# Softmax attention: value products of two key tiles in one block, and a third buffer for the exponentials

## The reference

```
qkv = x @ qkv_w.T + qkv_b          # q, k, v: 16 heads x 2048 x 8
p   = softmax(q @ k.T / sqrt(8))
out = (p @ v) @ proj_w.T + proj_b
x   = x + out
```

## Time and profile before

| | us |
|---|---|
| median of 3 runs | 1849.06 |
| lowest and highest | 1844.62, 1851.38 |
| the profiled execution | 1840.17 |
| its span | 1838.4 |
| mean granted clock of PE | 0.928 |

### The profile page before, as it was taken

How to read it: one execution, slowest core, us unless ns; L and a number is a source line. 1 busy time by engine, 2 the same in 40 slices (tenths; PEclk the granted TensorE clock), 3 DMA queues, 4 the chain that set the end, 5 groups by cost and what they waited for, 6 DMA issues and landing times. The chain is left out here.

```text
span 1838.4 us, 21584 instructions
## 1 busy us (share of the span) xinstructions
PE 1607.5 (87%) x7285; PEld 675.5 (37%) x7285; DVE 1352.3 (74%) x1951; ACT 856.2 (47%) x1493; POOL 222.4 (12%) x145
## 2 busy tenths in 40 slices
PE   6987589999999999999998799899984446589999
PEld 3433212222222222222223344466651112266665
DVE  5775798888888888888851777556666999745554
ACT  2443417777777777777776434322223000132221
POOL 2222300000000000000000122211100334201110
PEclk8998659999999999999999999899996767799999
DMA  6000310011001100120000000000000000000000
GB/s 171 4 0 1 124 30 8 15 28 37 12 15 28 33 15 15 28 32 10 2 2 1 1 0 0 1 1 0 0 1 0 0 1 0 1 1 6 6 6 7
DMA packets 32017, 29.42 MB, mean 16 GB/s; under 512 B 7789, under 2 KB 27033, under 8 KB 31929
## 3 DMA queue, kind: packets, MB, share of 16 engines
q1 hardware_dynamic: 31928, 28.31, 6.1%
HBM read 22.13 MB, written 4.19 MB: 14 GB/s over the span
## 5 line engine op out<-in xcount | busy, mean ns | idle before, releaser
L1350 DVE TENSOR_REDUCE mx<-ps 128x1 f32<-128x1024 f32 x512 | 603.1, 1219 | 108.9 <-PE ps L1262 107.6
L1338 ACT ACTIVATE xT<-ps 128x512 f32<-128x512 f32 x512 | 277.8, 598 | 123.4 <-PE ps L1285 117.0
L1262 PE MATMUL ps<-k,q 72*128 72x512 bf16 x1024 | 324.0, 399 | 11.0 <-DVE mx L1350 9.3
L1285 PE MATMUL ps<-q,k 84*128 84x512 bf16 x1024 | 311.7, 383 | 8.9 <-ACT xT L1338 6.4
L1338 ACT ACTIVATE xn<-ps 128x512 f32<-128x512 f32 x512 | 278.1, 601 | 83.9 <-PE ps L1285 79.1
L1285 PEld LDWEIGHTS ps<-q,k 84*128 84x128 bf16 x1024 | 96.4, 97 | 372.7 <-ACT xn L1338 152.6
L854 ACT ACTIVATE silu<-ps 128x512 f32<-128x512 f32 x144 | 85.3, 596 | 265.2 <-PE ps L827 261.8
L889 DVE TENSOR_TENSOR hid<-ps,silu 128x512 f32<-128x512 f32 x144 | 97.8, 689 | 90.2 <-PE ps L831 88.5
L827 PE MATMUL ps<-xT,ew 128*128 (+1 forms) x288 | 150.4, 604 | 6.4 <-PEq L1718 4.8
L817 PEld LDWEIGHTS ps<-ew,hid 128*128 128x128 f32 x1152 | 138.7, 192 | 30.6 <-issue 29.9
L831 PE MATMUL ps<-xT,ew 128*128 (+1 forms) x288 | 148.8, 599 | 0.0
(11 more groups left out here) (239 smaller groups left out, 1686.2 us busy)
## 6 DMA issues: line engine op xcount, KB each, us to landing
k<-k_parts SPq DMA_DIRECT2D x90, 64.0 KB
q<-q_parts SPq DMA_DIRECT2D x144, 32.0 KB
k<-k_parts SPq DMA_DIRECT2D x108, 32.0 KB
ew<-in_L_ffn_w_dram SPq DMA_DIRECT2D x2, 1024.0 KB
wraw<-in_L_ffn_w_dram SPq DMA_DIRECT2D x3, 512.0 KB, 6.7
q_parts<-part SPq DMA_DIRECT2D x4, 384.0 KB, 3.9
k_parts<-part SPq DMA_DIRECT2D x4, 384.0 KB, 2.6
v<-values SPq DMA_DIRECT2D x8, 144.0 KB, 6.1
```

What stands on the lines that cost most here:

```text
L1262: mm = nc.tensor.matmul(m.ps[:, S1B[2 * (i % 2) + kc % 2], :], queries, k1[:, h, kc * CHUNK:(kc + 1) * CHUNK], start=True, stop=True)
L1285: nc.tensor.matmul(m.ps[:, S2B[n % len(S2B)], :], k2[:, h, kt * P:(kt + 1) * P], q[:, qc, h, :], start=True, stop=True).then_inc(s2_ready, 1)
L1338: nc.scalar.activation(ex[kt % P_RING][:, h, :], m.ps[:, S2B[n % len(S2B)], :], ACT.Exp)\
L1350: nc.vector.reduce_max(mx[:, h, qt, kc:kc + 1], m.ps[:, 2 * (i % 2):2 * (i % 2) + 2, :], AX.XY)\
```

## The change

PE no longer runs a value block behind every tile but behind every odd tile, and then those of the two tiles one after the other. The exponentials get a third buffer, `ex2`, with memory of its own (four heads x 512 numbers per partition), and the buffer of a tile is now its running number over all units modulo 3, where it was the tile's number modulo 2. The copy of a unit's result on ACT stands behind the fourth exponential of the next unit's tile 0, not behind the third. Everything else, the first pass, the number of matmuls, the three PSUM banks of the scores and all transfers, stays as it is.

```
-P_RING = 2
+P_RING = 3
...
         ex = [m.xT[:, :].rearrange("p (h t) -> p h t", t=CHUNK),
-              m.xn[:, :, :].rearrange("p (h a) d -> p h (a d)", a=TPC)]
+              m.xn[:, :, :].rearrange("p (h a) d -> p h (a d)", a=TPC),
+              m.sb("ex2", [P, GH, CHUNK], stack=stack)]
...
                     last = nc.tensor.matmul(m.ps[32 * h:32 * h + VC, AVB, :], v[:, kt, h, :],
-                                            ex[kt % P_RING][:, h, :], start=(kt == 0), stop=(kt == TILES - 1),
+                                            ex[(u * TILES + kt) % P_RING][:, h, :], start=(kt == 0), stop=(kt == TILES - 1),
...
                     score(n + 5)
                     score(n + 6)
                     ahead(u, 2 * kt + 1)
-                    weigh(u, kt)
+                    if kt % 2 == 1:
+                        weigh(u, kt - 1)
+                        weigh(u, kt)
...
-                        nc.scalar.activation(ex[kt % P_RING][:, h, :], m.ps[:, S2B[n % len(S2B)], :], ACT.Exp)\
+                        nc.scalar.activation(ex[(u * TILES + kt) % P_RING][:, h, :], m.ps[:, S2B[n % len(S2B)], :], ACT.Exp)\
                             .then_inc(exped, 1)
-                        if kt == 0 and h == 2 and u > 0:
+                        if kt == 0 and h == 3 and u > 0:
                             store_out(u - 1)
```

## The result

The change made the kernel slower: 1880.82 us (median of 4 runs, 1874.44 to 1885.0) against 1846.84 (1841.06 to 1851.38), ratio 1.018, 95% interval 1.0146 to 1.0222. The profiled execution, at 1885.0 us the slowest of the four, has a span of 1883.2 us against 1838.4, mean granted clock 0.92 against 0.928.

What follows compares the result with a forecast made beforehand. PE's stream and ACT's exponential loop were both taken as close to binding, ACT's loop binding in the last 20 tiles. Terms summed to +24.7 us: 1864.9 against the profiled 1840.17, 1873.8 against the median 1849.06; range 1862 to 1890.

Steps and rivals of the forecast that it cites:

- the sum: All loop terms added: units 0 to 13 19.0, unit 14 to tile 11 1.2, last 20 tiles 4.5; together +24.7 us.
- rival B: Between two value blocks: the second block's weights are loaded in the open, +15 us, 1889; chance 0.13.
- The pair in the middle: Two tiles in the middle of a unit: 5.79 us against 5.64, +0.15 per pair.
- both waits: In a middle pair: first pass waits for DVE's reduction until 2.15 (costs 0.18), score 10 for exponential 7 until 3.19 (0.17).
- The unit: One unit's pairs added: 6 x 0.15 + 0.32 + 0 + 0.15 = 1.37 us more.
- tiles 12 and 13: Pair beside the empty first-pass slot: ends at 5.63 us, change 0.
- The seam: Place between two value blocks: bounds nothing or up to 0.12 us for eight weight loads; taken as nothing.
- Rival A: PE's stream alone sets the time: each pair 0.20 to 0.22 us shorter, -27 us, 1822; chance 0.09.
- Rival D: Third buffer doesn't do its work, ACT stands in the double block: 25 us more, 1899; chance 0.05 including the unseen.
- The copy: Start of a unit: copy before exponential 4 shifts everything up to score 10 by 0.33 us; difference +0.15.
- The last 20 tiles: Tiles without first pass, bound by ACT's loop: pair 5.19 us against 4.76, +0.43 for each of 10 pairs.
- score 6's: Before the change, score 6 waits for exponential 3: weights load at 1.08 us, just in time for its turn at 1.10.

Runs made afterwards that it cites:

- cut kernels: Kernel before (single blocks) and changed kernel (pairs), both with half of each exponential and reduction left out: 1820.88 us, ratio 0.9865, and 1792.08 us, ratio 0.9722.

## Why the prediction was right, and where it was short

It said 1873.8 us, range 1862 to 1890, slower; measured 1880.82. By the ratio the loss is 1.84% or 34 us (27 to 41), where the sum had 24.7. The account of the middle of the units came out to a few hundredths. That the total fell inside the range is in part luck: the sum was short by 9 us, and the range reached that far up only to take in rival B, which is false.

- *The pair in the middle.* 5.79 forecast, 5.79 in the trace, with both waits at their places (2.15 and 3.19 forecast, 2.14 and 3.19 found). The mechanism, the meeting of PE's stream with ACT's loop, is what the runs with shortened ACT and DVE show: pairs save 28.2 us against single blocks once both are out of the way.
- *The unit.* 1.37 us forecast, 1.44 found; tiles 12 and 13, taken at nothing, cost 0.05.
- *The seam.* Taken at nothing; it is nothing, the second block starts 0.86 to 0.87 behind the first. Rival B falls.
- *Rival A* (PE's stream alone, faster) fell as well, though its premise is true: 0.22 us per visit saved, against the 0.20 read from the gaps at entry and exit. The drain at a change of tiling mode that the Trainium skill speaks of (TensorEngine Tiling (Array Packing), Key Properties) agrees with the 0.22 us that the two cut kernels show per visit, though no run tells a drain from another cost of the change. The gain that follows from it alone did not come.
- *Rival D* (no help from the third buffer) did not apply, but its price was about right: 6.01 per pair measured without the buffer, and about 32 us above the changed kernel where 25 was written.
- *The copy.* Forecast to cost 0.33 us where it now stands; moving it back gave 0.29.
- *The last 20 tiles: the term that was mis-sized.* I wrote +0.43 for each of 10 pairs, at the clock of 1.00 that the earlier trace rows show. The first two pairs are at 5.20, as forecast. Then one takes 7.32 (with the copy in it) and six take 6.84, 1.64 us longer still, because the clock fell with PE's longer waits. That is about 11 of the 14.5 us by which the profiled loops (39.2) exceed the sum. How much of it an execution pays varies: the four of the changed kernel took 1885.0 and 1883.51 us at mean clocks of 0.920 and 0.921, and 1878.13 and 1874.44 at 0.925, while with single blocks in these tiles all four lay between 1867.8 and 1869.42. I had read the clock before the change and kept it for a stretch in which PE now waits longer at a time. The row has PE at 43.2 of 49 us there, where it was 99.0 of 100 in the middle, and that should have made a rival of it.
- *The start.* Before unit 0's copy 2.3 us more were lost than forecast. The first pair's two value blocks ran at 1.2 GHz (1.7 each), and the stretch from 270 to 280 has a clock of 0.55 against 0.93. No run tested this apart, but the profiles speak for a later rise with pairs. Where no work is left out, the granted clock goes to 1.00 54.4 to 56.7 us after the fill of `k` in the five kernels with single blocks, and 57.8 to 59.7 us after it in the five with pairs, one profile each. The loops up to the first copy took 97.8 to 99.3 us with single blocks and 100.4 or more with pairs, of which the copy's place makes up to 0.8. In the cut kernels the rise came equally early with both orders (50.1 and 49.4 us).
- *What holds ACT's loop in the last 20 tiles.* The prediction took the trace to show ACT's emptying of PSUM as the limit there. With seven banks and scores issued further ahead, a tile fell from 2.38 to 1.96 us with exponentials as long as before. So what held these tiles was that with three banks no score could be ready earlier, and not ACT's rate; ACT was busy 41.0 of 49 us.

Of the 44.8 us between the two profiled spans, 5.6 lie outside the loops. The fill of `k` started anywhere from 215.3 to 223.1 us in the kernels profiled, which are the same up to there. What sets it stays open.

## What to carry to other kernels

When an engine is 99% busy, a saving on it helps only as far as the engines that feed it can keep up with the shorter time: put the producers' loop and the engine's stream on one time axis and see which wait is just met, as score 6's was (1.08 against 1.10). Batching work that used to give a producer time to catch up asks for a deeper ring (more buffers in rotation) between the two, here PSUM banks; that this would have saved the pairs is an argument, for the deeper ring was only run with single blocks. The third buffer deepened the other ring, behind ACT. And where a change makes PE wait at more places in a row, price the clock with it: in the last 20 tiles the waits cost 4 us by themselves and about 12 through the clock.

## What the runs showed of the hardware

- Value blocks of 9 columns in four column groups cost 0.22 us per visit beyond their stream when 128-column matmuls stand on both sides, at 2.4 GHz (a unit of 45.26 us against 43.49 in the cut kernels, over 8 visits); between two such blocks it is nothing (the second starts 0.86 to 0.87 behind the first).
- PE's clock fell to 1.2 GHz without any single idle time above 0.6 us: in pairs with one of 0.26 us and four of 0.10 behind one another, five scores starting 0.64 and 0.49 apart instead of 0.22. It did so in both profiles of such pairs, beginning at different ones, and now and then in the last 20 tiles of the pairs with two buffers. The same pairs with the waits filled kept 2.4 GHz in their profile. With single blocks, one idle time of 0.26 us per 2.38 us tile, it fell in none of four profiles.
- Behind a wait of 2.0 us for a transfer, four scores took 1.89 us instead of 1.04; in the kernel with the same banks but without that wait, the clock stayed at 1.00.
